# Layer norm in chunks of 512 tokens, its inverse root off ScalarE, and FFN weights in pieces: one change to a two-layer kernel on one core

## What is computed

```python
def _layernorm(x, axis=-1, eps=1e-05):
    return (x - mean(x)) / jnp.sqrt(var(x) + eps)
...
x = x + 0.5 * L0_ffn(_layernorm(x))     # 16 experts, top 4, plus a shared one
x = x + L0_attn(_layernorm(x))          # one causal head, rank 32, values of width 256
...                                     # and so on, layer by layer
x = x + 0.5 * L1_ffn(_layernorm(x))     # silu(g * gate_s) * (u * up_s), then down, 704 wide
x = x + L1_attn(_layernorm(x))          # 16 causal heads of 128 with rotary embedding
x = x + 0.5 * L1_ffn(_layernorm(x))
```

## Time and profile before

| what | value |
|---|---|
| median of 3 runs (lowest, highest) | 2454.03 us (2451.86, 2455.87) |
| profiled execution: its own time | 2449.4 us |
| profiled execution: span | 2447.6 us |
| busy PE, PEld, DVE, ACT, POOL | 85%, 76%, 67%, 58%, 36% |
| blocks that a norm opens, start of each in the span | 0, 222, 364, 579, 717, 2313 us |

### The profile page before, as it was taken

One profiled execution on the slowest core, in us unless ns is written; L12 is line 12 of the kernel. 1 busy time (PEld: TensorE's weight loads), 2 busy tenths in 40 slices (PEclk: granted clock), 3 DMA queues, 4 the chain that ended last, 5 costly groups with the idle time before them and its releaser, 6 DMA issues. The chain is left out here.

```text
span 2447.6 us, 42392 instructions
## 1 busy us (share of the span) xinstructions
PE 2073.9 (85%) x14632; PEld 1862.0 (76%) x14632; DVE 1646.4 (67%) x3777; ACT 1413.6 (58%) x3646; POOL 887.4 (36%) x746
## 2 busy tenths in 40 slices
PE   4953886872977999999999999999999999999688
PEld 3842784761867888888888888888888888888668
DVE  6465766475347777777777777777777777777643
ACT  3342553342335776766766767667667677676532
POOL 1463001564223343343343343433433434324232
PEclk9975897975988999999999999999999999999989
DMA  4064002063000000000000000000000000000100
GB/s 138 1 182 96 1 8 95 30 178 98 1 33 3 10 3 8 10 3 8 10 3 5 4 12 5 3 12 5 4 10 8 4 10 4 7 1 1 40 9 26
DMA packets 43986, 66.81 MB, mean 27 GB/s; under 512 B 5632, under 2 KB 29440, under 8 KB 43648
## 3 DMA queue, kind: packets, MB, share of 16 engines
q1 hardware_dynamic: 37632, 55.71, 7.0%
q0 software_dynamic: 6144, 8.39, 2.0%
HBM read 48.89 MB, written 15.20 MB: 26 GB/s over the span
## 5 line engine op out<-in xcount | busy, mean ns | idle before, releaser
L1003 ACT ACTIVATE phase_pt_hi<-phase_ring 128x512 fp32r<-128x512 f32 (+3 forms) x680 | 345.7, 536 | 205.3 <-PE phase_ring L988 201.9
L963 ACT ACTIVATE phase_p<-phase_scores,phase_bias 128x512 f32<-128x512 f32 (+3 forms) x680 | 416.5, 625 | 74.0 <-DVE phase_bias L951 72.4
L1008 DVE TENSOR_TENSOR phase_pt_lo<-phase_ring,phase_pt_hi 128x512 fp32r<-128x512 f32 (+3 forms) x680 | 394.7, 603 | 76.3 <-ACT phase_pt_hi L1003 76.2
L944 DVE TENSOR_REDUCE phase_peaks<-phase_scores 128x1 f32<-128x512 f32 (+3 forms) x680 | 396.2, 603 | 55.6 <-PE phase_scores L936 27.1
L988 PE MATMUL phase_ring<-sb_ident,phase_p 128*128 128x128 f32 x2312 | 348.0, 275 | 39.0 <-DVE phase_pt_lo L1008 30.3
L115 PE MATMUL phase_y<-phase_pt_hi,phase_v_hi 128*128 128x256 f32 x1152 | 333.3, 289 | 0.0
L988 PEld LDWEIGHTS phase_ring<-sb_ident,phase_p 128*128 128x128 f32 x2312 | 263.0, 141 | 81.8 <-issue 47.7
L117 PE MATMUL phase_y<-phase_pt_hi,phase_v_lo 128*128 128x256 f32 x1152 | 322.1, 280 | 0.0
L116 PE MATMUL phase_y<-phase_pt_lo,phase_v_hi 128*128 128x256 f32 x1152 | 321.6, 279 | 0.0
L1749 POOL TENSOR_TENSOR phase_straight<-phase_rot,phase_rope 64x512 f32<-64x512 f32 x128 | 163.6, 1278 | 373.5 <-ACT phase_rot L1628 373.5
L933 PE MATMUL phase_scores<-phase_k_hi,phase_q_hi 128*128 128x512 f32 (+2 forms) x640 | 253.6, 396 | 9.9 <-POOL phase_k_lo L1758 5.4
(11 more groups left out here) (271 smaller groups left out, 5480.6 us busy)
## 6 DMA issues: line engine op xcount, KB each, us to landing
phase_raw_up<-expert_up SPq DMA_DIRECT2D x32, 352.0 KB, 3.1
phase_raw_dn<-expert_down SPq DMA_DIRECT2D x32, 256.0 KB, 2.7
y_rows<-phase_zero SPq DMA_DIRECT2D x8, 512.0 KB, 7.8
xn_rows<-phase_ln_xn SPq DMA_DIRECT2D x8, 512.0 KB, 3.2
phase_ln_xn<-y_rows SPq DMA_DIRECT2D x8, 512.0 KB, 5.5
phase_raw_qk<-qk SPq DMA_DIRECT2D x16, 256.0 KB, 2.6
phase_raw_up<-up SPq DMA_DIRECT2D x4, 704.0 KB, 6.7
sb_x<-x SPq DMA_DIRECT2D x4, 512.0 KB, 5.6
```

The lines of the kernel that those rows point to most:

```text
L944: dve.tensor_reduce(self.peaks[:, t % 2, c:c + 1], self.scores[:, at:at + self.width(t, c)], AX.X, ALU.max).then_inc(*self.peaked.one)
L963: act.activation(self.p[:, at:at + width], self.scores[:, at:at + width], ACT.Exp, bias=self.bias[:, t % 2:t % 2 + 1], accum_out=self.sums ...
L1003: act.activation(hi, value, ACT.Copy).then_inc(*self.t_hi.one)
L1008: dve.tensor_tensor(lo, value, as_f32(hi), ALU.subtract).then_inc(*self.t_lo.one)
```

## The change

Norm works by chunks of four tiles and each of its steps is a call that a block places where it wants: `dve_measure(c)`, `pool_power(c)` (POOL: variance to the power -0.5), `dve_root(c)` (four small steps of the Newton correction and `shift` = -mean * rstd), `act_scale(c)` (ACT: x * rstd + shift, four instructions), `pe_turn`, `act_turn`, `dve_turn`. The consumers wait for `norm.lo` of their own chunk. There is no square root and no reciprocal of it. `y` has its own buffer and weights are loaded ahead of it. In both attentions the norm's steps are in `plan_order`, and their transposes use the ring. Attention0's bias is added by POOL. Gated loads and splits its up weights in six pieces on ACT and DVE, folds 0.5 * `ds` into the down weights, does "down" of a chunk after piece 1 of the next one, row tile by row tile (two PSUM buffers), and stores the result by row tile.

```diff
 class Norm:
+    def dve_measure(self, dve, c):
+        if self.first:
+            dve.wait_ge(*self.x_in[c][tag])
+        if self.add_y:
+            if c % 2 == 0:
+                dve.wait_ge(*self.y_in[c][tag])
+                dve.tensor_tensor(x, x, self.y[:, c], ALU.add).then_inc(*self.grown[0].one)
+            dve.wait_ge(*self.grown[c % 2][key])
+        for t in range(4):
+            done = dve.bn_stats(self.stats[:, t, :], x[:, t, :])
+        for t in range(4):
+            done = dve.bn_aggr(self.mv[:, c % 2, t, :], self.stats[:, t, :])
+        dve.tensor_scalar(self.var[:, c % 2], self.mv[:, c % 2, :, 1], EPS, None, ALU.add).then_inc(*self.varied.one)
+    def dve_root(self, dve, c):
+        dve.wait_ge(*self.powered[key])
...
+        dve.scalar_tensor_tensor(shift, mean, -1.0, rstd, ALU.mult, ALU.mult).then_inc(*self.shifted.one)
+    def pool_power(self, pool, c):
+        pool.wait_ge(*self.varied[self.tag, c])
+        pool.tensor_tensor(self.rstd[:, 4 * c:4 * c + 4], self.var[:, c % 2], self.half[:], ALU.pow).then_inc(*self.powered.one)
+    def act_scale(self, act, c):
+        act.wait_ge(*self.shifted[self.tag, c])
...
+        for j in range(4):
+            done = act.activation(self.xn[:, c % self.rooms, j], self.core.x[:, t, :], ACT.Identity,
+                                  bias=self.shift[:, t:t + 1], scale=self.rstd[:, t:t + 1])
 class Route, pe:
         for c in range(NCH):
+            if c + 1 < NCH:
+                for k in range(HK):
+                    pe.wait_ge(*self.norm.lo[tag, c, k])
+                    self.norm.pe_turn(pe, c + 1, k, self.down_ps[:, k, :])
...
+            if c:
+                self.pe_logits_back(pe, c - 1)
 class Route, act:
         for c in range(NCH):
+            for k in range(HK):
+                self.norm.act_turn(act, c, k, self.down_ps[:, k, :])
+            if c:
+                self.act_logits(act, c - 1)
+            if c + 1 < NCH:
+                self.norm.act_scale(act, c + 1)
 class Attention0:
-        order = [(what, c) for c in range(NCH) for what in ("state", "action")]
+        order = [("stats", 0), ("weights", "ws", "wa"), ("root", 0), ("scale", 0), ("stats", 1), *turned(0), ("root", 1), ("scale", 1),
+                 ("state", 0), ("action", 0), ("weights", "wo0"), ("stats", 2), *turned(1), ("score", 0, 0, 0), ("peak", 0, 0), ("exp", 0, 0),
+                 ("root", 2), ("scale", 2)]
         for t in range(NT + 1):
+            c = t // 4 + 1
+            if c < NCH:
+                n = c + 1
+                order += {1: [("state", c), ("action", c)], 2: turned(n) + [("stats", n + 1)] if n + 1 < NCH else turned(n) if n < NCH else [],
+                          3: [("root", n + 1), ("scale", n + 1)] if n + 1 < NCH else []}.get(t % 4, [])
 class Attention1:
+        order = [("load_qk", 0), ("stats", 0), ("root", 0), ("scale", 0), ("load_wv", 0), ("stats", 1), *turned(0), ("project", 0, 0),
+                 ("root", 1), ("scale", 1), ("finish", 0, 0), ("project", 0, 1), ("stats", 2), ("score", 0, 0, 0), ("peak", 0, 0), ("exp", 0, 0)]
...
+                if h == 0 and t % 4 == 0 and t + 4 < NT:
+                    n = t // 4 + 1
+                    order += turned(n)
+                    if n + 1 < NCH:
+                        order += [("root", n + 1), ("scale", n + 1)]
+                    if n + 2 < NCH:
+                        order.append(("stats", n + 2))
 class Gated, pe:
+            for m in range(I1M):
+                self.pe_up(pe, c, m)
+                if m == 1 and c:
+                    self.pe_down(pe, c - 1)
+                if m == 2 and c + 1 < NCH:
+                    for k in range(HK):
+                        pe.wait_ge(*self.norm.lo[self.tag, c, k])
+                        self.norm.pe_turn(pe, c + 1, k, self.turn_ps[:, k, :])
+        self.pe_down(pe, NCH - 1)
 class Gated, dve (ACT's and POOL's parts are cut):
+        norm.dve_measure(dve, 0)
+        self.dve_up_weights(dve, 0)
+        norm.dve_root(dve, 0)
+        self.dve_up_weights(dve, 1)
...
+        self.dve_up_weights(dve, 2)
+        norm.dve_measure(dve, 1)
+        self.dve_up_weights(dve, 3)
+        norm.dve_root(dve, 1)
...
+        dve.tensor_tensor(self.raw_dn[:], self.raw_dn[:], self.ds[:].unsqueeze(1).broadcast_to([P, I1M, H]), ALU.mult).then_inc(*self.scaled.one)
+        for c in range(NCH):
+            for m in range(I1M):
+                self.dve_piece(dve, c, m)
+                if m == 2 and c == 0:
+                    dve.tensor_tensor(self.dn_lo[:], self.raw_dn[:], as_f32(self.dn_hi[:]), ALU.subtract).then_inc(*self.down_w_lo.one)
+                if m == 1 and c:
+                    self.dve_add(dve, c - 1)
...
+                if m == 3 and c + 2 < NCH:
+                    norm.dve_measure(dve, c + 2)
+                if m == 4 and c + 2 < NCH:
+                    norm.dve_root(dve, c + 2)
+        self.dve_add(dve, NCH - 1)
```

More of the change, by code:

```diff
@@ new lines, in act_piece @@
+    def act_piece(self, act, c, m):
+        tag, rows = self.tag, self.rows(m)
+        act.wait_ge(*self.up[tag, c, m])
+        if old := self.before(c, m):
+            act.wait_ge(*self.acted[old])
+        act.activation(self.gate[rows, m % 2, :], self.up_ps[rows, m % 2, :], ACT.Silu, scale=self.gs[rows, m:m + 1]).then_inc(*self.gated.one)
+        act.wait_ge(*self.acted[tag, c, m])
+        if c and (m >= 2 or c >= 2):
+            act.wait_ge(*self.down[tag, c - 1 if m >= 2 else c - 2, 3])
+        act.activation(self.h_hi[rows, self.slot(c, m), :], self.mul[rows, m % 2, :], ACT.Copy).then_inc(*self.hi.one)
```

590 lines of the change are left out of this document (314 added, 276 removed).

## The result

The changed kernel takes 2474.21 us (median of 4, 2472.14 to 2478.36) against 2453.91 us for the kernel before beside it: ratio 1.0085, 95% interval 1.0067 to 1.0102. It is slower by 20 us (0.8%, clear of the noise) where 35 us less was forecast. Its profiled execution has a span of 2470.3 us against 2447.6, so the traces differ by 22.7.

A forecast was written before the change was run, and what follows sets the result against it. DVE bounds the lead-ins, PE the bodies. Gated1 -15.9, gated0 -13.0, Attention0 -8.4, Attention1 -1.1 and Routes +3 sum to -35.4 us: 2414.0 profiled, median 2418.6, range 2410 to 2428 (chance 0.48).

The forecast's parts named there:

- three signs of being wrong: PE waits in every chunk of a body, power over 2 us, or Attention1 over 5 us off.
- rival C: Norms: the power on POOL is dear, each us over 0.5 costs 6, over 3 up to 24; slower from 4; chance 0.05.
- rival D: Attention bodies: Identity needs another table than Exp's, two loads per scaling, so the removal gives nothing; chance 0.01.
- rival E: Route0: POOL's first call of a freshly loaded function waits about 6 us, making 2425; chance 0.05.
- the down products' rows: Gated's down products: priced at 0.12 us each, sixty under 7 us, with no term for dropped padding.
- slow start: Gated0's first products: PE starts at the slow clock, 2.0 us more for about ten matmuls.
- exposed once per norm: Every norm: the power, taken as 0.5 us, is exposed only in chunk 0, where DVE has nothing else.
- gated0's start: Gated0: first product at 594.7 against 618.70, 24.0 us earlier, 16 us after the block's start.
- Route's chain: Routes: chunk period 5.8 or 6.8 us, last logits at 38.9 to 43.1; +2 for route0, +1 for route1.
- Attentions: Attention0 -8.4 us (-3 to -13), first exponential 20.1 earlier; Attention1 -1.1 (-6 to +4), first projection 7.8 earlier.
- rival A: Attention and gated bodies: each of 10 chunk insertions costs 1.5 us more, saving 20, so 2434; chance 0.20.

The follow-up runs named there:

- e1: The changed kernel with the half piece of Gated's down projection padded with zeros to 128 rows again: 2459.41 us.
- e9: The changed kernel without the four DVE steps that refine the reciprocal root between power and shift: 2451.49 us.
- e7: The changed kernel with each of the 24 powers on POOL done twice: 2491.01 us.
- e3: The changed kernel with Route reordered: next chunk's root and following statistics before the current rests on DVE, next scaling before previous logits on ACT: 2457.93 us.
- e2: The changed kernel with Attention1's root and scaling of chunk 1 behind the first head's finish, its power ahead of the first rope products: 2470.44 us.
- e8: The changed kernel with the edits of e1, e2 and e3 together: 2440.38 us.
- e5: e1 with chunk 1's norm steps and the down weights' scaling in Gated spread behind the pieces of chunk 0: 2461.80 us.
- e6: The changed kernel with Attention0's sums of y all on DVE, first exponential ahead of chunk 1's root and scaling and chunk 2's statistics: 2473.27 us.
- e11: e8 with chunk 0's scaling in every norm done by DVE instead of ACT: 2437.02 us.

## Why the prediction was wrong

The sum had -35.4 and the trace has +22.7. Of the 58 us between, the Gated blocks make 27, the attentions 20, the Routes 8, Experts' scatter 3. Of the prediction's three signs of being wrong only one came: Attention1 is over 5 us off (10.0); in the Gated bodies chunks 1 and 2 have no wait over 0.3 us, and the power took 1.02 us, under the 2 us named. No rival reaches the measured time either: the nearest, C, needs a power of over 4 us.

**What held.** The bound: DVE in the lead-ins, PE in the bodies. Gated1's first product came 11.0 us after the start (10 forecast). Gated0's waits in chunk 0, 2.46, 1.02 and 2.23, are the 2.7, 1.1 and 2.5 of the prediction, and the last chunk's 0.79 + 1.46 the forecast 2.6. Chunks 1 and 2 have one wait of 0.30 each. (In other profiles of the same Gated code the wait of 2.46 is 2.5 to 3.7, so the near match of that one is partly luck.) Transposes at 0.12 are near (eight delay the next product by 0.79). No ACT table had to be loaded for Identity (rival D); the trace has 6 table loads of 1.28 us instead of 15. No power had to wait for its first call: 1.02 us at 12.73 (rival E). For the 6 us that the Trainium skill, GPSIMD Engine Reference, Instruction dispatch, gives for the first call of a freshly loaded function this decides nothing: POOL's MODIFY_POOL_CONFIG stands at 1.8 us and POOL is idle from there for 10.9 us, so a load could lie in that time unseen.

**Step missed: the down products' rows (10.4 us by the rows; e1 measured 14.8).** The prediction priced the new order of the down products by its waits, took 0.12 for each product (sixty under 7 us, with the earlier trace rows), and had no term for the padding that the diff drops. The rows of the kernel before show only 128-row products there, so the price was unknown and should have been bounded; it had no line at all. By block e1 gives 13.4 of the Gated blocks' 27 back; the later starts (3.0 and 0.9) and the slow start below make some 5 more, and about 9 stay open, in part falls of the clock inside chunk 0 (0.67 from 639.61 to 644.61).

**Step wrong: "exposed once per norm".** The power was mis-sized (1.02 for 0.5) and so was ACT's scaling (2.08 for 1.4; one is 0.59 busy and they follow at 0.50, where the row of 476 ns had one scale and no bias). But the size alone, 1.2 us in six norms, is 7 us. What failed is the exposure. The sum took chunks 1 to 3 as hidden in a body. Three runs say otherwise: leaving out 19.2 us of root steps gave 20 to 23 us (e9); Attention1's power, root and scaling of chunk 1 lie in PE's wait of 8.24 us; and a second power, 1.05 us, in 24 places cost 16.8 us, 11 of these us in the Gated blocks (e7). By rival C's own words each us over 0.5 costs 6, and chunks 1 to 3 join in only from about 3 us; at 2.07 us they already do, in Gated with waits of 1.3. The Routes are the exception: e7 cost them about 1 us together. A reason can be read in the earlier trace rows, which the prediction quoted, though no run tests that by itself: where DVE is 18.12 of 20 us busy, a step put in front of a peak isn't beside other work.

**Step mis-sized: gated0's start.** The first product came at 18.8 instead of 15.8: chunk 0 of y was summed 1.5 us later than forecast, the power took 1.43 beside DVE where 0.5 was forecast, the scaling 2.08 where 1.4 was.

**Step mis-sized: Route's chain.** Period 5.8 or 6.8 was forecast, 6.1 to 7.3 measured, and logits at 44.07 where 38.9 to 43.1 were the bounds; two Routes cost 10.6 instead of 3. The prediction had followed the order as it stands and found the right chain; that this order need not be, and that e3's makes both Routes shorter than in the kernel before (122.5 and 112.3 against 124.3 and 118.2), it did not ask.

**Attentions.** First exponential -17.3 where -20.1 was forecast, Attention1's first projection -5.8 for -7.8: sized well. The body took the rest: Attention0's took back 19.0 instead of 11.7. That is rival A, with more than its 1.5 per insertion. In Attention1 the queue that was overlooked is POOL's: the prediction put the norm steps at "2", and did not ask what the power is queued behind (the wait for the rope's input and two rope products, 2.6 us) and who is queued behind the root and the scaling (the first head's finish). e2 halved that wait and got 2 to 4 back.

**Clock.** The slow start was forecast as 2.0 in gated0 and measured 2.9 (24 products in 8.38 instead of 5.5 us). What was missed is that it falls again within the bodies behind some waits (0.57 from 724 to 732, 0.91 from 780 to 815), and that the same code behind the same waits can keep it, as gated1 of e8 did and gated0 of e8 did not. That share can't be separated by these runs from the waits themselves.

**Still open.** What the removal of the square root from ScalarE is worth by itself was not tried; nor what makes the clock fall after the same two waits, always with 64-row products among the next ones and in three of ten cases without; nor what the early start alone costs an attention, with the ring and the bias left as they were.

## What to carry to other kernels

Starting a pipeline with its first chunk turns a lead-in, in which long operations run alone, into short dependent steps inside a body; count each of those steps as on the path for every chunk unless a row shows the engine idle for longer than the step at that very place. A step that is just hidden now is exposed as soon as it gets longer (e7), so ask for the slack too. Read the diff for what it drops as closely as for what it adds: four memsets of zeros per Gated block were worth 15 us. When a gain fails to come, move the same step and shrink it: if moving gives nothing (e5, e6) and shrinking gives the step's whole length (e9), it is price and not order; if moving gives it all (e3), it is order.

## What the runs showed of the hardware

- A product of 64 rows behind one of 128 starts 0.21 us after it instead of 0.12, and the next one 0.22 after that, at the high granted clock; the same on the way back.
- Behind the same two waits (0.79 and 1.46 us) the last 57 down products took 9.7 us (granted clock 0.82) or 11.1 us (0.69) in fourteen of fourteen cases with mixed rows, and with 128 rows 7.1 us (1.00) in seven of ten and 8.3 to 8.6 us (0.80 to 0.83) in three.
- A 128x4 power on POOL takes 1.01 us alone and up to 2.53 beside DVE at work (e5); a 0.16 us DVE step takes up to 2.33 beside a POOL sum of 2.37.
- Four scalings of 128x256 take 2.08 us on ACT (Identity with scale and bias by partition) and 1.38 on DVE (e11).
- Leaving out 3.2 us of DVE steps in Attention1 (e9) shortened the block by 6 to 10: 1597.8 against 1603.8 to 1607.7.
